# Attention: scores, mix, transpositions in place of scores, transpositions, mix on TensorE

## The reference, cut to what matters

```
raw = einsum('bhqd,bhkd->bhqk', q, k) / scale      # 2 batches, 32 query heads, 8 key heads
masked = raw + mask                                # 512 queries x 1024 keys
attn = softmax(masked, axis=-1)
out = einsum('bhqk,bhkd->bhqd', attn, v)           # depth 128
```

## Time and profile before

| What | us |
|---|---|
| median of 3 runs | 3483.4 |
| lowest and highest run | 3466.51, 10604.78 |
| the profiled execution | 3467.62 |
| its span in the profile | 3465.7 |

### The profile page before, as it was taken

The page is one execution under the profiler, slowest core; times in us unless marked ns, Lnnn a source line. Parts: engine busy times, 40 slices in busy tenths (PEclk is TensorE's granted clock), DMA queues, the critical chain, the costliest instruction groups (busy, mean ns, idle before and its releaser), DMA issues. The chain is left out here.

```text
span 3465.7 us, 45672 instructions
## 1 busy us (share of the span) xinstructions
PE 3012.4 (87%) x14140; PEld 2414.5 (70%) x14144; DVE 2882.1 (83%) x4335; ACT 2154.2 (62%) x2742; POOL 911.5 (26%) x547
## 2 busy tenths in 40 slices
PE   5888858788769999999999899995656999999999
PEld 4777747566548888888888676763425777777787
DVE  7999969679759999999999799998584788888753
ACT  4777747567657777777777588884142565655531
POOL 3777746226111111111111055550000101101100
PEclk9999979899989999999999899997677999999999
DMA  3333432342331111111111244330022221212211
GB/s 111 128 112 116 133 133 91 122 139 91 128 119 53 55 46 61 49 59 49 58 49 49 88 130 132 121 109 31 0 97 67 68 67 61 85 61 67 73 49 52
DMA packets 170336, 286.81 MB, mean 83 GB/s; under 512 B 11712, under 2 KB 98752, under 8 KB 170176
## 3 DMA queue, kind: packets, MB, share of 16 engines
q1 hardware_dynamic: 160960, 268.24, 23.3%
q10 hardware_dynamic: 9216, 16.78, 1.3%
HBM read 196.64 MB, written 88.34 MB: 82 GB/s over the span
## 5 line engine op out<-in xcount | busy, mean ns | idle before, releaser
L898 ACT ACTIVATE at_pth<-at_t 128x512 fp32r<-128x512 f32 x512 | 282.1, 597 | 250.4 <-PE at_t L991 250.4
L941 DVE CUSTOM_DVE_ANT_0 at_sc<-at_s,at_mk 128x1024 f32<-128x1024 f32 x256 | 312.1, 1219 | 61.6 <-issue 40.0
L205 ACT ACTIVATE ff_nf_above<-ff_nf_raw,sharp 128x1024 f32<-128x1024 f32 x255 | 291.6, 1148 | 94.0 <-DVE ff_nf_val L220 74.4
L957 DVE TENSOR_TENSOR at_ptl<-at_t,at_pth 128x512 fp32r<-128x512 f32 x512 | 328.1, 682 | 1.1 <-ACT at_pth L898 1.1
L220 DVE SCALAR_TENSOR_TENSOR ff_nf_val<-ff_nf_above,ff_nf_val 128x1024 f32<-128x1024 f32 x238 | 308.2, 1295 | 21.2 <-ACT ff_nf_above L205 18.6
L205 ACT ACTIVATE pq_nf_above<-pq_nf_raw,sharp 128x1024 f32<-128x1024 f32 x240 | 263.1, 1113 | 98.9 <-DVE pq_nf_val L220 83.5
L205 ACT ACTIVATE ou_nf_above<-ou_nf_raw,sharp 128x1024 f32<-128x1024 f32 x240 | 267.3, 1117 | 77.8 <-DVE ou_nf_val L220 62.4
L888 ACT ACTIVATE at_pr<-at_sc,at_sm 128x1024 f32<-128x1024 f32 x256 | 295.2, 1153 | 21.8 <-DVE at_sm L944 15.1
L991 PE MATMUL at_t<-ident,at_pr 128*128 128x128 f32 x2048 | 273.1, 275 | 16.2 <-DVE at_ptl L957 16.0
L117 PE MATMUL ff_g<-yT_h,ff_guh 128*128 128x512 f32 x704 | 286.3, 407 | 0.0
L991 PEld LDWEIGHTS at_t<-ident,at_pr 128*128 128x128 f32 x2048 | 235.4, 140 | 67.4 <-DVE at_ptl L957 28.0
(11 more groups left out here) (210 smaller groups left out, 8091.0 us busy)
## 6 DMA issues: line engine op xcount, KB each, us to landing
ff_raw<-dq SPq DMA_DIRECT2D x63, 512.0 KB, 4.0
pq_raw<-in_L_xattn_wq SPq DMA_DIRECT2D x32, 512.0 KB, 5.4
q_d<-pq_res SPq DMA_DIRECT2D x32, 512.0 KB, 2.6
at_qraw<-q_d SPq DMA_DIRECT2D x64, 256.0 KB, 2.7
o_d<-at_ot ACTq DMA_DIRECT2D x64, 256.0 KB, 2.0
ou_oraw<-o_d SPq DMA_DIRECT2D x32, 512.0 KB, 3.9
ou_wraw<-in_L_xattn_wo SPq DMA_DIRECT2D x32, 512.0 KB, 4.0
pq_nf_raw<-in_L_ffn_w SPq DMA_DIRECT2D x16, 512.0 KB, 5.3
```

The source lines that it names most:

```text
L205: act.activation(self.above[:, (s + j) % 2, 0:width], self.raw[:, s, 0:width], ACT.Relu, bias=self.sharp[:, j:j + 1], scale=SHARP).then_in ...
L898: act.activation(pt[0][:, h % 2, j * HALF:(j + 1) * HALF, (n % QT) * P:(n % QT + 1) * P], t_ps[:, j], ACT.Copy).then_inc(t_hi.sem, 1)
L941: dve.tensor_tensor_reduce(sc[:, n % 2], s_ps[:, n % 2], mk[:, bb * QT + n % QT], 1.0, NEG, ALU.add, ALU.max, sm[:, n % 2, 0:1]).then_inc( ...
L957: dve.tensor_tensor(pt[1][sl], t_ps[:, j], f32(pt[0][sl]), ALU.subtract).then_inc(t_lo.sem, 1)
```

## The change

In each step TensorE takes the mix before the transpositions. The three pieces, their lags and their waits are unchanged, as is every other engine's list.

```diff
@@ -1007,7 +1007,7 @@
                     last.then_inc(mixed.sem, 1)
 
             def do_step(b, i, n):
-                for lag, act_on in ((0, scores), (2, turn), (MIX_LAG, mix)):
+                for lag, act_on in ((0, scores), (MIX_LAG, mix), (2, turn)):
                     if exists(b, i, n - lag):
                         act_on(b, i, n - lag)
```

## The result

The changed kernel takes 3526.9 us in the median of four runs (3525.67 to 3535.69), against 3475.36 in the median of the kernel before, without its one slow run of 10604.78 us (3479.38 with it); the ratio is **1.0148**, 95% interval 1.0132 to 1.0164. It is slower, by less than 2%. The profiled execution is the longest of the four (3535.69, span 3533.9).

What follows compares the result with a forecast made beforehand. The prediction saw TensorE, with VectorE nearly full too, bounding the attention stage (943.6 and 894.8 of 966 us). Terms 52.3 + 1.4 + 2.7 = +56.4 us on 3467.6 gave 3524 us, range 3485 to 3547.

Steps and rivals of the forecast that it cites:

- The floor: TensorE's steady step in the attention stage: stays 3.61 us in either order, so the change earns nothing there.
- term 1: Mix opening a head waits on TensorE for the low part of the transposition issued 2.03 us before: 0.46 us net.
- term 2: GpSimd's query subtraction holds VectorE's scaling before a head's mix: net wait 0.83 us a head, 63 heads +52.3 us.
- a shared rate: VectorE's scaling and GpSimd sharing their port at half rate: the head's net wait would be 0.66 us, an estimate.
- the list of what would show it: Signs in the trace: mix waits 65 to 75 us, transposition waits under 15, over 60 scalings near 1.3 us.
- term 3: Key and value steps: GpSimd's subtractions hold the scaling, 1.35 us a pair in place of 1.17, 15 pairs +2.7 us.
- The tail: Stage's end, the 64th case: mix(251) goes before the last transposition, shifting the last head's chain, +1.4 us.
- The loop jumps: VectorE's four loop jumps, late by 2 us each: costed at nothing; -4 if the new slack took it.
- The rival with the key's scaling first: Key step: scaling starts before GpSimd, so the key costs nothing: +36 us, 3504; chance 0.14.
- The rival of no hold: Query's subtraction falls clear of the scaling: +33 us, 3501, or +13, 3480, without the key's hold; chance 0.20.
- that of a covered wait: Not slower: scores cover the mix's wait, only the relief of transposition waits remains: -17.4 us, 3450; chance 0.05.
- that of a loss above 2%: Value's hold also ends in a head's wait (15 x 1.5 = 23 us): +79 us, 3547; chance 0.13.

Runs made afterwards that it cites:

- e6: Kernel before the change, with GpSimd waiting for VectorE's scaling ahead of all its subtractions (queries, keys, values): ratio 0.9957 to before, stage 928.3 us.
- e7: Changed kernel with the mix one step later (lag 7 for 6) and GpSimd waiting for the scaling before all subtractions: ratio 0.9939 to before, stage 923.2 us.
- e4: Changed kernel with GpSimd waiting for VectorE's scaling before all subtractions (queries, keys, values): ratio 1.0030 to before, stage 960.0 us.
- e9: The same kernel as e6, measured again with more rounds: ratio 0.9949 to before, stage 930.7 us.
- e1: Changed kernel with the mix one step later (lag 7 in place of 6): ratio 0.9964 to before, stage 934.8 us.
- e5: Kernel before the change (old order) with the mix one step earlier (lag 5 in place of 6): ratio 1.0728 to before, stage 1183.9 us.

## Why the prediction was right

Term by term, each against its own step:

- **The floor.** TensorE's cycle of 3.61 in either order: measured 57.81 for 16 steps in e6 and e7, and 58.35 where the steps have their second length of 3.65.
- **The head's wait alone (term 1).** 0.46 net for a head was forecast; 0.47 to 0.53 is measured (e4 against e9, and by groups against e6). I had given back 0.12 for the restart of a drained TensorE, which was a little much: the six products then take 1.26 instead of 1.36 (1538.80 to the next transposition's load at 1540.06), so 0.10.
- **The query's hold (term 2).** The places in the frame were forecast within 0.06: GpSimd -0.11 to 1.17 (measured -0.17 to 1.11), scaling at 0.38 (0.39), low part at 1.63 (1.58), mix load at 2.98 (2.93). The net value was 0.83 and is 0.87 by the mask distances. The hold of a whole instruction against a shared rate decides 0.17 of this; the scaling ended 0.55 after GpSimd (1537.53 against 1536.98). The Trainium skill (SBUF - State Buffer, Who interferes with whom) has the rule that the one which starts second blocks, and this agrees with it and not with a shared rate. Why the scaling ended 0.55 after GpSimd, and not its whole 0.75, is not shown. The count was off in the list of what would show it: 42 held scalings, not over 60. My own steps for term 3 had it that the scaling behind the key's is not held, which takes 15 away; four more stand behind the loop jumps, where VectorE is late enough to miss GpSimd, and the rest at the stage's two ends. The waits of the mix sum to 77.7 us in 64 waits, against 65 to 75 forecast, and those of the transposition to 14.2, against under 15.
- **Keys and values (term 3).** 1.35 a pair in place of 1.17: the 16 steps of a group take 62.55 now; with four heads of 0.87 over 57.8 that leaves 1.3. The key's scaling took 2.82 (forecast 2.89), and the wait behind it is the 1.8 of the trace (forecast 1.65). The price of before was read too low: I took 0.58 each from the one step in the earlier trace rows, but most such steps take 4.27 or 4.31, and a pair costs 1.28 in the median. So the term came out near nothing and not at +2.7.
- **The tail** was forecast at +1.4. From the last mask operation to the end of the last copy it is 14.4 before and 14.7 after, +0.3. **The loop jumps** were put at nothing. A group with one is 1.7 us longer than the mean of the others before and 2.1 after, so some +1.4 for the four. This miss, and those of the tail and of term 3, are 1 to 3 us each and partly cancel, which is luck.
- **Sum.** +56.4 forecast; +54.3 measured in the stage with its tail. Against the profiled execution of before, 1.0148 is +51.

The rival with the key's scaling first is a real mechanism: e1 shows it. It did not come up in the changed kernel, where GpSimd was first by 0.12 or 0.13 in all 15 cases; the forecast had 0.06. That was the narrowest point of the prediction, worth 20 us, and it could have gone the other way. The rival of no hold fell by 42 scalings, that of a covered wait by e4, and that of a loss above 2% since the value's hold ends in no wait of TensorE.

## What to carry to other kernels

When blocks of an in-order engine are swapped, count for each consumer the time from its producer's block, before and after: the work between them is the cover. Here a head's mix came 3.61 + 0.77 = 4.38 us after the transposition that it needs, and 2.03 after the swap, while the detour over two other engines takes 2.6. Then look at what else moves with it: the same swap slid VectorE's scaling under GpSimd's subtraction, and this second effect was two thirds of the first (38.7 - 16.4 = 22 us against 32). An order and a lag belong together: each alone lost, both together gained, because one was limited by a result not yet there and the other by a buffer not yet free.

## What the runs showed of the hardware

- VectorE's scaling and GpSimd's subtraction hold each other up, in either direction: 0.75 became 1.27, 1.54, 1.82, 2.55 or 2.82 with GpSimd first, and GpSimd's 2.41 became 2.69, its 1.28 became 1.54, with the scaling first. With GpSimd first the scaling ended 0.55 us after it whether it had begun 0.12 us behind GpSimd's start (changed kernel) or 1.41 (kernel before), which a shared rate would not give. VectorE's mask operation and low part did not change: 1.21 to 1.23 and 0.67 to 0.69 us throughout the stage, beside GpSimd too. A wait of GpSimd for the scaling's semaphore removed all of the hold and cost nothing measurable.
- With a wait of about 2.8 us on TensorE at each head (e5), the granted clock went to 0.50 instead of 1.00 for several microseconds at 30 of 63 heads, with products 0.43 us apart instead of 0.23. With the waits of 0.9 to 1.9 us of the changed kernel no such fall began between the stage's first mask operation and its last.
- At a granted clock of 1.00 the same step of TensorE takes 3.61 or 3.65 us in long rows (e6: 122 and 108 steps). Nothing here shows why.
